# Sandwich kernel: the gathered query rows are turned back in their own PSUM pair and divided first, and a layer-norm step of four tiles moves one slot

## What is computed

```
q, k, v = split_heads(h @ W + b)                  # h = layernorm(x); 2 x 16 heads, 1024 x 32
ctx = local_attention(q, k, v)                    # blocks of 128 queries, windows of 256 keys
idx = [0] + top 62 by norm(q) + [t - 1]
g_ctx = softmax(q[idx] @ k^T / sqrt(d)) @ v       # 64 chosen rows of each head see all 1024 keys
ctx[idx] = g_ctx
x = x + layernorm(ctx)
x = x + layernorm(moe(layernorm(x)))
```

## Time and profile before

| | us |
|---|---|
| median of 3 runs | 823.47 (823.22 to 826.71) |
| the profiled execution's own time | 823.6 |
| its span | 821.8 |
| PE busy | 777.9 (95%) |
| DVE busy | 563.3 (69%) |
| ACT busy | 422.9 (51%) |
| POOL busy | 146.1 (18%) |

### The profile page before, as it was taken

How to read it: one execution, slowest core, us unless ns; L and a number is a source line. 1 busy time by engine, 2 the same in 40 slices (tenths; PEclk the granted TensorE clock), 3 DMA queues, 4 the chain that set the end, 5 groups by cost and what they waited for, 6 DMA issues and landing times.

```text
span 821.8 us, 13879 instructions
## 1 busy us (share of the span) xinstructions
PE 777.9 (95%) x5060; PEld 651.3 (79%) x5060; DVE 563.3 (69%) x1196; ACT 422.9 (51%) x839; POOL 146.1 (18%) x229
## 2 busy tenths in 40 slices
PE   6999999999999999898999999999999999999994
PEld 4787887777777777676877887999999999887883
DVE  5764897578987566676588545466776666758666
ACT  5464352455656566666544244566675666723120
POOL 3300010410112014232344432000000000013122
PEclk9999999999999999999999999999999999999998
DMA  7789465975676788772339622676787776546444
GB/s 234 228 277 347 164 204 174 268 221 164 173 218 167 195 216 223 210 197 93 104 133 322 238 95 90 193 214 209 220 241 227 236 232 212 170 149 200 152 154 141
DMA packets 117492, 162.39 MB, mean 198 GB/s; under 512 B 17364, under 2 KB 65236, under 8 KB 117424
## 3 DMA queue, kind: packets, MB, share of 16 engines
q1 hardware_dynamic: 113840, 153.54, 61.8%
q0 software_dynamic: 3584, 7.97, 3.2%
HBM read 107.24 MB, written 55.05 MB: 197 GB/s over the span
## 4 chain that ended last, share of the span: by engine, by line
PE 65%; DVE 18%; DMA 5%; ACT 4%; issue 3%; POOL 1%; SPq 0%; POOLq 0%; DVEq 0%; ACTq 0%
PE bank L163 43%; PE wide L163 17%; DVE MX L160 4%; PE wide L167 3%; PE bank L167 2%; DVE SG L160 2%; DMA XX<-scr_xd 2%; DVE STC L281 1%; DMA scr_q<-hl 1%; DVE GC L153 1%; DMA scr_qtok<-H2A 1%; ACT PTG L145 1%; DMA H2A<-scr_oe,FG 1%; ACT PT L157 1%; DVE SIL L149 1%
## 5 line engine op out<-in xcount | busy, mean ns | idle before, releaser
L163 PE MATMUL wide<-W2H,HH 128*128 128x512 f32 x308 | 101.8, 396 | 0.5 <-ACT OUTR L145 0.5
L160 DVE TENSOR_REDUCE MX<-wide 128x1 f32<-128x192 f32 (+1 forms) x128 | 77.6, 647 | 20.9 <-PE wide L163 20.9
L157 ACT ACTIVATE PT<-bank 128x512 f32<-128x512 f32 x128 | 73.4, 593 | 29.1 <-PE bank L163 29.0
L157 ACT ACTIVATE SIL<-bank 128x256 f32<-128x256 f32 (+1 forms) x72 | 32.7, 454 | 98.1 <-PE bank L163 97.8
L149 DVE TENSOR_TENSOR SIL<-bank,SIL 128x256 f32<-128x256 f32 (+1 forms) x72 | 36.9, 512 | 64.0 <-ACT SIL L157 63.3
L163 PE MATMUL bank<-XT,W13H 128*128 128x256 f32 (+1 forms) x336 | 76.6, 322 | 0.0
L145 ACT ACTIVATE HH<-SIL 128x256 fp32r<-128x256 f32 (+1 forms) x72 | 35.2, 489 | 66.6 <-DVE SIL L149 66.6
L163 PEld LDWEIGHTS wide<-W2H,HH 128*128 128x128 f32 x308 | 58.6, 190 | 13.3 <-ACT OUTR L145 1.3
L149 DVE TENSOR_TENSOR HH<-SIL,HH 128x256 fp32r<-128x256 f32 (+1 forms) x72 | 37.0, 514 | 45.9 <-ACT HH L145 37.7
L163 PE MATMUL wide<-W2L,HH 128*128 128x512 f32 x168 | 66.5, 396 | 0.8 <-DVE W2L L149 0.7
L163 PEld LDWEIGHTS bank<-XT,W13H 128*128 128x128 f32 x336 | 55.0, 188 | 4.7
(11 more groups left out here) (256 smaller groups left out, 2010.4 us busy)
## 6 DMA issues: line engine op xcount, KB each, us to landing
R<-in_L_ffn_W_dram SPq DMA_DIRECT2D x48, 512.0 KB, 5.6
scr_q<-hl SPq DMA_DIRECT2D x16, 512.0 KB, 4.3
scr_k<-hl SPq DMA_DIRECT2D x16, 512.0 KB, 4.1
R<-in_L_ffn_sw_dram SPq DMA_DIRECT2D x12, 512.0 KB, 5.4
QSe<-scr_q SPq DMA_DIRECT2D x36, 128.0 KB, 3.7
KSe<-scr_k SPq DMA_DIRECT2D x36, 128.0 KB, 3.7
R<-_attn_hidden_states_dram SPq DMA_DIRECT2D x16, 256.0 KB, 3.9
scr_qtok<-H2A SPq DMA_DIRECT2D x16, 256.0 KB, 3.8
```

The source lines that it names most:

```text
L157: return do("act", lambda g: g.activation(dst, src, fn, **kw), after)
L160: return do("dve", lambda g: g.tensor_reduce(dst, src, AXX, op), after)
L163: return do("pe", lambda g: g.matmul(ps, a, b, start=start, stop=stop, skip_group_check=True), after, mark=mark)
```

## The change

`global_back` no longer takes a bank of `ST_`. It writes into the second bank of the wide pair in which `global_values` left its result; that pair is given back to `W_` by the last DVE product of `global_finish` instead of by ACT's copy into `OS`. In slot k = 1 `global_back` and `global_finish` now come ahead of `local_turn` and `local_finish`. And `H_AT` moves three steps of tiles 0 to 3: `h_mean2` from 7 to 8, `h_h2` from 8 to 9, `h_turn` from 10 to 11. Tile t's `h_mean2` thereby stands in slot k = 0 of group 11 + t, its `h_h2` in k = 1 and its `h_turn` in k = 3.

```
@@ global_values, global_back, global_finish
                 m_c = copy("act", os[:, 0:P], w[:, 0:P], [m_o] + sfree)
-                W_.busy[g_["wi"]].append(m_c)
                 g_["os"] = (si, os, m_c)
+                g_["back"] = (g_["wi"], w[:, 512:576])
...
-                ti, tb, tfree = ST_.take()
-                g_["back"] = (ti, tb)
-                g_["m_t"] = mm(tb[:, 0:64], os[:, 0:P], twice[:, :], True, True, [m_c, m_two] + tfree, mark=True)
+                g_["m_t"] = mm(g_["back"][1], os[:, 0:P], twice[:, :], True, True, [m_c, m_two], mark=True)
...
-                ti, tb = g_["back"]
+                wi, tb = g_["back"]
...
-                ST_.busy[ti].append(m_f)
+                W_.busy[wi].append(m_f)
@@ the table
-            H_AT = {0: h_mean, 5: h_x1, 7: h_mean2, 8: h_h2, 10: h_turn}
+            H_AT = {0: h_mean, 5: h_x1, 8: h_mean2, 9: h_h2, 11: h_turn}
@@ slot_of
+                if k == 1 and i > 0:
+                    global_back(i - 1)
+                    global_finish(i - 1)
                 if g >= 5 and g % 4 == 1:
                     local_turn((g - 5) // 4)
                     local_finish((g - 5) // 4)
-                if k == 1 and i > 0:
-                    global_back(i - 1)
-                    global_finish(i - 1)
```

## The result

| | before | after |
|---|---|---|
| median of 6 runs | 825.83 (823.22 to 828.01) | 832.63 (830.81 to 834.37) |
| the profiled execution's own time | 823.6 | 834.26 |
| its span | 821.8 | 832.5 |
| PE's mean granted clock over the span | 0.989 | 0.979 |

The ratio is 1.0085, with a 95% interval of 1.0058 to 1.0112: slower. The forecast was 829.4 us, 823 to 833, and slower by over 0.5% as the likeliest case.

What follows compares the result with a forecast made beforehand. PE, busy nearly throughout, was taken to bound the kernel. Terms -2.3 + 0.3 - 0.7 - 3.1 + 6.8 + 4.8 = +5.8 us on the profiled 823.6 gave 829.4 us, range 823 to 833.

Steps and rivals of the forecast that it cites:

- The sum: All terms against the profiled execution before: +5.8 us, giving a span of 827.6 and a time of 829.4 us.
- Its case: The forecast's likeliest outcome: slower by over about 0.5%, chance 0.50.
- The swap: Slot k = 1: `SG` starts at T + 1.66, T starting the first product behind `global_scores`; -2.3 us over 11 groups.
- The +0.3 us behind group 15: Behind group 15 the router's first product waits for `GC` instead of starting at once: +0.3 us.
- The cover of 0.24 us for the wide pair: Slot k = 1: `GC` frees the wide pair at T + 0.93, before `row_max` asks at about T + 1.17.
- The second mean of tile 0: Slot k = 7 of group 10: `MX` now goes ahead of DVE's wait for POOL's add; -0.7 us.
- The late row: PE's wait for DMA `QSe<-MR` before group 12's scores, plus slow clock, shrinks to 0.3 us: -3.1 us.
- one rival: The late row and slow clock behind it stay or turn up in another group: 832.5 us, chance 0.10.
- The stall of `H2A`: Groups 11 to 14: L942 behind `SG` delays ACT's `H2A`, PE stands 2.3 us, `row_shift` 1.70 us later; +6.8 us.
- The clock: PE's clock falls after most of the four new gaps in groups 11 to 14, 1.2 us each: +4.8 us.
- The rival that ACT's queue lets `PT` pass the waiting `H2A`: ACT between `PT` of k = 1 and `PG`: stall covered, gains stand alone, -5.8 or 817.8 us, chance 0.13.

Runs made afterwards that it cites:

- e8: Kernel before with the new order of slot k = 1 alone, product still in a single bank, old step table; ratio 0.9973 to before.
- e7: Kernel before with the product with `twice` moved into the wide pair alone, old order and old step table; ratio 1.0035 to before.
- e6: Kernel before with the three W2 loads issued in groups 13, 14 and 15 instead of 8, 9 and 11; ratio 0.9970 to before.
- e2: Kernel before with the new table of steps alone (8, 9, 11); ratio 1.0144 to before.
- e5: e1 with the three W2 loads issued in groups 13, 14 and 15 instead of 8, 9 and 11; ratio 0.9944 to before.
- e1: Swap only: kernel before with the wide buffer and new order in slot k = 1, old table of steps; ratio 0.9969 to before.
- e3: Kernel after with `h_h2` of tiles 0 to 3 at the head of slot k = 1, ahead of divisions and `SG`; ratio 1.0014 to before.
- e9: Kernel after with the three W2 loads issued in groups 13, 14 and 15; ratio 1.0065 to before.
- e10: e9 with nine products that nobody reads ahead of the transposes of `H2A`, keeping PE busy; ratio 1.0026 to before.
- e4: Kernel after with nine products that nobody reads ahead of the transposes of `H2A`, keeping PE busy; ratio 1.0040 to before.

## Why the prediction was right

The sum was +5.8 us; the median moved by 6.8 and the profiled execution shows +10.7. Its case was the right one, and one step of it failed. That the median of 832.63 us lies inside the range, by 0.4 us, owes something to luck: the term of the clock was too small by more than 3 us.

- **The swap, -2.3 us: right, a little too small.** `SG` starts at T + 1.59, not T + 1.66, and the groups are 0.28 us shorter, not 0.21. Up to group 9 the kernel gained 2.63 us. That only the order does it (e8) was in the working: the 0.21 us came from DVE's chain alone. The +0.3 us behind group 15 came too: the router's product waited 0.35 us for `GC`. The cover of 0.24 us for the wide pair held in the new order and broke in the old one (e7).
- **The second mean of tile 0, -0.7 us: right in size by luck.** The path from `SG` of group 10 to that of group 11 fell from 14.51 to 13.70 us. But the move is not what shortens it. With the old order of the slot it took 13.57 us in the old place (e6) and 13.58 in the new (e2); with the new order 13.27 to 13.73 in the old place (e5, e1, e8) and 13.27 to 13.77 in the new (e3, e9, e10). The wait for `MX` came with a late POOL step in the execution of before; why POOL was late there stays open.
- **The late row, -3.1 us: half right.** In group 11 it did not come back. It came in group 9 instead, as one rival had it, at 1.15 us. That group took 14.70 us, 0.78 more than before, which leaves about 2.6 us of the 3.4 that group 11 had lost:

```profile
304.31 0.51 PE L163 MATMUL bank<-WQH,WKH 97*128 97x256 f32 x2 [1.15 <-DMA WQH<-MR]
```

  The cause that I gave, bulk loads ahead of the small DMA, is borne out by e5 and e6 and is not the whole of it (e2).
- **The stall of `H2A`, +6.8 us: right in mechanism, place and size.** Predicted: `H2A` at T + 3.2, PE idle 2.3 us, `row_shift` at T + 6.78, 1.70 us more a group. Measured: T + 3.09, 2.22 us, T + 6.79 (e10) and 15.79 - 14.08 = 1.71 us. e3 shows that the place of L942 alone decides it.
- **The clock, +4.8 us: the step that failed.** The price of one fall, 1.2 us, was near the measured 1.36. But I counted at most one fall a group, only behind the four gaps, and some of them not at all. All four came, and the clock was low for longer than that: the clock of group 11 is 0.82 and that of group 14 is 0.83, against 0.90 for a single fall. By the groups this is worth about two falls more, and the term comes to some 8.5 us (4 x 1.36, 1.34 in group 11 and 1.7 in group 14). In group 11 the clock stayed low for twice as long as in e9, whose PE had the same gap: these are the kernel after, with the transposes of `H2A` at 327.20 us, and e9, with them at 326.13.

```profile
327.00:333.00 6.00, 5.80 (x30) 3.71 (x31) 1.13 (x3) 3.84 (x9) 0.00 (x0) 0.50 0.69 184
```

```profile
330.00:333.00 3.00, 3.00 (x34) 2.80 (x29) 1.73 (x5) 2.07 (x5) 0.00 (x0) 1.00 0.04 10
```

  That made 18.54 us of 17.20. Why it did so in this execution and not in e9 was not settled. In group 14 a second fall came behind two shorter waits:

```profile
388.90 0.61 PE L163 MATMUL bank<-late 97*128 97x128 f32 x3 [0.68 <-ACT PT L157]
...
390.38 0.30 PE L167 MATMUL bank<-ident,MX 128*72 128x128 f32 x1 [0.64 <-DVE MX L160]
```

  They are not of the change's making. The kernel before has the same two in its group 14, where the clock stayed at 1.00:

```profile
380.33 0.60 PE L163 MATMUL bank<-late 97*128 97x128 f32 x3 [0.68 <-ACT PT L157]
381.81 0.30 PE L167 MATMUL bank<-ident,MX 128*72 128x128 f32 x1 [0.64 <-DVE MX L160]
```

  With these waits the clock fell in e3, e6, e7 and e8, where PE never waits for `H2A`, and stayed up in before, e1 and e5. Group 14 of e6 (the kernel before with the later loads) took 16.64 us instead of 14.96:

```profile
369.39:386.03 16.64, 14.74 (x117) 10.99 (x117) 10.84 (x26) 10.28 (x23) 4.35 (x5) 0.90 0.47 145
```

  So of the 5.0 us that group 14 took more than before, where 2.9 were predicted, about 1.7 go to a fall that kernels without the stall have as well. It is not shown whether the change made it likelier; it came in all six profiled executions of kernels with the stall (after, e2, e4, e9, e10) or the moved turns (e3).
- The rival that ACT's queue lets `PT` pass the waiting `H2A` fell with the 3.23 us of idle ACT ahead of `H2A`; the in-order rule that the Trainium skill states (TensorE: Matmul & The Clock Gate, Architectural detail) agrees with that row.

The median lies 6.8 us above that of the kernel before, the profiled execution 10.7 above its own: the execution of before that I summed against was among the quick ones of its kernel, and that of the kernel after, at 834.26 us, among the slow ones.

## What to carry to other kernels

Before moving a step in queues that keep their order, ask on each engine what the moved instruction now stands behind, and who stands behind the one that waits for it: a 0.15 us step put behind a long reduction cost 2 us of PE's path four times over. Price the gap twice, once as waiting and once as the slow clock that follows. And try the parts of a change alone: here one half of one part held all the gain, its other half was a loss by itself, and the remaining part alone lost about five times what the good half gained (1.4% against 0.3%). Before a loss in a group is put down to a change, look for the same waits in the kernel before.

## What the runs showed of the hardware that I had not expected

A single gap in otherwise dense work is enough for the clock to fall: each of the four gaps of 2.2 us brought it to 0.50, nine products that nobody reads kept it at 1.00 at all four of them, and each fall cost about 1.35 us. Two shorter waits of 0.68 and 0.64 us, with some 0.8 us of work between them, brought the clock down in some kernels and not in others, the waits being the same; there the fall cost about 1.7 us.

And the small DMA of a row, 4 KB, can set PE back when 512 KB loads are issued some 5 to 7 us ahead of it. Of the eight profiled kernels that issue such loads in groups 8, 9 and 11, six (before, after, e1, e3, e7, e8) lost 1.1 to 2.1 us so in group 9 or 11, and e2 and e4 did not; e4 waited 1.3 us for a row in group 7, ahead of these loads. With the loads moved to groups 13 to 15, no wait for a row was longer than 0.7 us in any of the four kernels.
